# An attention and expert kernel: the expert part is spread in small steps between the turns of the attention loop

## The chip, the cores and the metric

The kernel runs on one core of a Trainium2 chip. The metric is the device time of one execution in microseconds (us). Five engines work side by side, each in the order of its own instruction list, and wait for each other through semaphores: PE (TensorE, matrix multiplies into the accumulators called PSUM, here one tile `ps` of eight banks of 512 f32 columns), ACT (ScalarE), DVE (VectorE), POOL (GpSimd) and SP (SyncE, which here only issues DMAs).

## The reference

For x of 2048 tokens by 128 features, normalised to xn, the output is x plus an attention of 16 heads of 8 features plus a mixture of 8 experts with the top 2 chosen per token.

```python
q, k, v = (proj(W) * mod for W in (Wq, Wk, Wv))              # 16 heads, 8 features each
scores = einsum('bhid,bhjd->bhij', q, k) / sqrt(D)
scores = scores * cos(2 pi (i - j) / S)
w = softmax(scores); w = (w + roll(w, 1, axis=-1)) / sqrt(2)
attn = einsum('bhij,bhjd->bhid', w, v) @ Wo
# experts: a small router picks 2 of 8 per token, each expert is
h1 = x_rep @ w1[e].T; a, g = split(h1); he = silu(a) * g @ w2[e].T     # 704 and 352 hidden
out = x + attn + sum over the two chosen experts of score * he
```

## The kernel before

The cosine factor is folded into the operands: each head has 16 rotated rows for q and for k, written as an f16 high part and an f16 rest to a scratch tensor in DRAM (`qk_parts`) and loaded head by head as 49 rows (`qa`, `ka`). Scores are computed transposed, as 64 tiles a head of 128 keys by 512 queries, 1024 tiles in all. The exponential (ACT, L581) writes a tile in f32 to `probs` (the tensor `big`), and four tiles together (a quad) are multiplied with the values of the head, `vh` (PE, L1098), on four column groups of PE at once.

The work runs in stages, all written out by hand for each engine:

1. The layer norm, the transposes of xn, the router's projection, the values, the expert weights' transposes (24 blocks, PE L926 and L928, taken out by ACT L518 to L521), and the router itself on DVE.
2. The rotated projections (PE L950, DVE L717), their split in two f16 parts (ACT L532, DVE L711), squares (ACT L537) and the stores to `qk_parts` (SP L339). At the same time POOL scatters the token rows, one indirect DMA for each of 32 columns of slots (L444), into expert order (`slots_x`).
3. 39 expert tiles of 128 rows (`run_tiles`). For each: SP loads rows, PE turns them (L959), multiplies with the two halves of w1, 352 columns each (L981, L986), ACT applies Silu (L557), DVE multiplies (L738), PE turns the result (L964), DVE copies it (L733), PE multiplies with w2 (L974), ACT copies (L553), POOL stores to `slots_y`. Stage 3 also holds, beside some tiles, the steps that rank the heads and make the shift rows of the softmax.
4. Attention. PE's loop runs over groups g of three score tiles (`GROUP_OF = 3`, 342 groups): `scores(g)` waits for the exponential of group g-2, then come a `max_job` (only for the two heads that need exact maxima: 128 jobs, 11 a head from head 1, each reduced by DVE L771), and the quads whose tiles are ready. POOL copies the next head's values (`head_values`) and gathers the experts' results beside it.
5. The output projection, the sum, and the stores.

The waits that decide between stages are PE's own order and these:

```python
after(pe, exp_done, g - 1)                       # scores(g)
pe.wait_ge(exp_done, groups_for(tiles[-1] + 1))  # weighted_values(w)
pe.wait_ge(vh_ready, p + 1)                      # first quad of head p
```

Of the kernel before, what the change touches and what calls it, by code (L numbers as in the profile page):

```python
# [30 lines left out]
F32 = mybir.dt.float32  # L31
# [21 lines left out]
TAIL = (GROUPS - 1) * GROUP  # L53
FP = NF * P
ROWS = 2 * D
KQ = 1 + 3 * ROWS
HALF = S // 2
CREDIT = 2
TURNED = 1
GROUP_OF = 3  # L60
RING = 2 * GROUP_OF
PROBS = 5 * GROUP_OF
PER_HEAD = NT * NC
SCORE_TILES = H * PER_HEAD
SCORE_GROUPS = -(-SCORE_TILES // GROUP_OF)
QUADS = PER_HEAD // NC
O_BANKS = (6, 7)
# [3 lines left out]
JOBS_A_HEAD = 11  # L71
JOB_QUAD = 6
ISQ8 = float(1.0 / np.sqrt(D))
# [8 lines left out]
PROJ_BANKS = (4, 5, 0, 1)  # L82
SUM_BANKS = (4, 6, 7, 0)
EARLY = 4
# [3 lines left out]
ONES = 3  # L88
# [3 lines left out]
SQUARES_AT, RANK_AT, ROW_AT, TURN_AT, ORDER_AT = 2, 4, 6, 7, TAIL - 1  # L92


def build(nc, x, Wq, Wk, Wv, Wo, phase, amp, wqkv, w1, w2, ident_in, desc_in, cs_in, sel_in, tri_in, below_in, count_in, heads_in, earlier_in, out):
    scratch = nc.dram_tensor("qk_parts", [2, H, 2, ROWS, S], F16, kind="Internal").ap()
    shift_rows = nc.dram_tensor("shift_rows", [H, S], F16, kind="Internal").ap()
    whole = nc.dram_tensor("whole_qk", [2, H, ROWS, S], F32, kind="Internal").ap()
# [7 lines left out]
    with ExitStack() as ctx:  # L106
# [3 lines left out]
        def sem(name):  # L110
# [7 lines left out]
        probs = big[:].rearrange("p a n -> p (a n)")[:, 0:PROBS * CW].rearrange("p (a n) -> p a n", n=CW)  # L118
        store = sb("store", [P, 10 * S], F16)
        parts = store[:, 0:8 * S].rearrange("p (a b n) -> p a b n", a=4, b=2)  # L120
        attn = store[:, 2 * S:4 * S].bitcast(F32).rearrange("p (t d) -> p t d", d=DM)

# [4 lines left out]
        total = gathered[:, 0, :, :]  # L127
        cs = sb("cs", [P, S], F32)

        hid = cs[:, 0:2 * FP].rearrange("p (a f) -> p a f", a=2)  # L130
        hidT = cs[:, 2 * FP:4 * FP].rearrange("p (a f s) -> p a f s", a=2, f=NF)
# [53 lines left out]
        silu = pair[:].rearrange("p t e j -> p (t e j)")[:, 0:2 * F].rearrange("p (a f) -> p a f", a=2)  # L185
# [33 lines left out]
        proj_ps, rot_ready, v_ps, v_ready, ones_ready = (sem(n) for n in ("proj_ps", "rot_ready", "v_ps", "v_ready", "ones_ready"))  # L219
        hi_ready, parts_ready, scratch_wr = (sem(n) for n in ("hi_ready", "parts_ready", "scratch_wr"))  # L220
# [6 lines left out]
        xgT_ps, xgT_ready, a_ready, g_ready, silu_ready = (  # L227
            sem(n) for n in ("xgT_ps", "xgT_ready", "a_ready", "g_ready", "silu_ready"))
        pad_ready, hid_ready, hidT_ps, hidT_ready, y_ready, y_copied, gather_ld, y_added = (
            sem(n) for n in ("pad_ready", "hid_ready", "hidT_ps", "hidT_ready", "y_ready", "y_copied", "gather_ld", "y_added"))  # L230
# [6 lines left out]
        whole_ld, whole_wr, whole_cs = (sem(n) for n in ("whole_ld", "whole_wr", "whole_cs"))  # L237
# [14 lines left out]
        def run_tiles(eng, tile, beside):  # L252


            for n in range(2 * GROUP):
                tile(n, n % GROUP, False)
                beside(n)
            with eng.Fori(2, GROUPS - 1) as g:
                for k in range(GROUP):
                    tile(g * GROUP + k, k, False)  # L260
            beside(TAIL - 1)
            for n in range(TAIL, TILES):
                tile(n, n % GROUP, n == TILES - 1)
                beside(n)
# [11 lines left out]
        def groups_for(n):  # L276

            return (n - 1) // GROUP_OF + 1
# [9 lines left out]
        def jobs_before(p):  # L288

            return min(max(p - 1, 0) * JOBS_A_HEAD, JOBS)  # L290

# [6 lines left out]
        def _(sp):  # L298
# [10 lines left out]
            for src, at in ((phase, 0), (amp, 1)):  # L309
                for g in range(2):  # L310
                    for half in range(2):
                        sp.dma_start(ang[64 * half:64 * half + 64, at, g:g + 1],
                                     src[8 * g:8 * g + 8, :].rearrange("h (d o) -> (h d) o", o=1)).then_inc(phase_ld, 16)
                sp.dma_start(ang[:, at, 2:3], src.rearrange("h (d o) -> (h d) o", o=1)).then_inc(phase_ld, 16)


            for b in range(2):
                for f, (f0, rows) in enumerate(FCH):
                    sp.dma_start(w1raw[0:rows, NF * b + f, :, :],
                                 w1[:, F * b + f0:F * b + f0 + rows, :].rearrange("e p h -> p e h")).then_inc(w_ld, 16)  # L320
            sp.dma_start(w2raw, w2.rearrange("e p f -> p e f")).then_inc(w_ld, 16)
            for dst, src in ((tri, tri_in), (below, below_in), (count, count_in)):
                sp.dma_start(dst[:], src).then_inc(route_ld, 16)
            sp.dma_start(cs[:], cs_in).then_inc(cs_ld, 16)

# [38 lines left out]
            def load_rows(m, half):  # L364
                after(sp, xgT_ps, m * 2 - 2)
                sp.dma_start(xg[:, 2 * half:2 * half + 2, :], tiles_x[:, bass.ds(m * 2, 2), :]).then_inc(xg_ld[half], 16)

            for i in range(3):
                store_parts(i)
            sp.wait_ge(scattered, 2 * NT * 16)  # L370
            sp.wait_ge(rot_ready, 16)
            for m in range(4):
                load_rows(m, m % 2)
            store_parts(3)
            for m in range(4, 6):
                load_rows(m, m % 2)
            with sp.Fori(3, GROUPS) as g:
                for half in range(2):
                    load_rows(g * 2 + half, half)
# [11 lines left out]
            for r in range(EXACT):  # L391
                load_operands(head_at(PLAIN + r), qe[:, r, :], ka[:, 2 + r, :], exact_ld)
# [832 lines left out]
```

## Time and profile before

| | us |
|---|---|
| median of 3 runs | 709.84 (708.99 to 710.26) |
| the profiled execution, as timed | 707.88 |
| its span, first to last instruction | 706.1 |
| PE busy | 621.4 (88%) |
| ACT busy | 550.1 (78%) |
| DVE busy | 220.7 (31%) |
| POOL busy | 93.3 (13%) |

The page's slices show PE and ACT at nine tenths or more from about 220 us to 690 us, the attention. Before that ACT and DVE are lightly used, and around 60 to 90 us PE does nothing. A busy PE is not a PE at its peak, since the ends of its matmuls are modelled. The profiled execution is 1.96 us (0.3%) under the median; of its 707.88 us, 1.78 us lie outside the span.

### The profile page before, as it was taken

Reading aid. Unit: us, or ns where it says so; the run is one execution under the profiler, and the core shown is the slowest. Engines: PE = TensorE matmul, PEld = TensorE weight load, DVE = VectorE, ACT = ScalarE, POOL = GpSimd, SP = SyncE. Lnnn points to the kernel's source line nnn. Section 1 sums busy time; section 2 is a strip of 40 time slices with the busy share of each in tenths; the row PEclk is TensorE's granted clock in tenths of the full one; section 3 lists DMA queues with packets and bytes.
Section 4 is the critical chain, followed back from the end, with each engine's and each line's share of the span. In section 5 each row is a group of like instructions: output and inputs, shape, how many; then the busy total and the mean of one; then the engine's idle time right before and its main releaser. Section 6 shows DMA issues by size and latency. Waiting matters only on the chain.

```text
span 706.1 us, 11470 instructions
## 1 busy us (share of the span) xinstructions
PE 621.4 (88%) x4151; PEld 201.4 (29%) x4152; DVE 220.7 (31%) x462; ACT 550.1 (78%) x530; POOL 93.3 (13%) x109
## 2 busy tenths in 40 slices
PE   3984057999989999999999999999999999999995
PEld 3841034677751111111111111111111111111113
DVE  7578024334420031423233142331414232005003
ACT  1466024233358999999999999999999999999992
POOL 2038720111110101010010101101010000000000
PEclk9998568899998999999999999999999999999999
DMA  4934321111141101011010101101010010000002
GB/s 129 313 121 148 120 62 66 45 45 59 48 131 47 43 5 46 16 31 36 12 46 1 47 16 31 43 3 46 1 46 25 19 35 1 3 1 1 1 0 63
DMA packets 33828, 34.44 MB, mean 49 GB/s; under 512 B 6092, under 2 KB 27878, under 8 KB 33650
## 3 DMA queue, kind: packets, MB, share of 16 engines
q1 hardware_dynamic: 30786, 27.01, 13.3%
q0 software_dynamic: 2992, 6.76, 2.9%
q8 instruction: 33, 0.54, 0.3%
q14 instruction: 17, 0.14, 0.1%
HBM read 21.14 MB, written 12.58 MB: 48 GB/s over the span
## 4 chain that ended last, share of the span: by engine, by line
PE 60%; ACT 18%; issue 13%; DVE 7%; SPq 2%; DMA 0%; ACTq 0%; DVEq 0%
PE ps L1098 23%; ACT big L581 16%; PE ps L1081 15%; PE ps L981 4%; PE ps L974 4%; PE ps L986 3%; DVE m L771 2%; PE ps L964 2%; SPq L339 2%; PE ps L1116 2%; PE ps L1105 1%; PE ps L915 1%; PE ps L906 1%; DVE big L717 1%; PE ps L959 1%
## 5 line engine op out<-in xcount | busy, mean ns | idle before, releaser
L581 ACT ACTIVATE big<-ps 128x1536 f32<-128x1536 f32 x342 | 471.2, 1459 | 11.9 <-PE ps L1081 4.5
L1098 PE MATMUL ps<-big,vh 128*32 128x512 f32 x2048 | 274.1, 607 | 0.1
L1081 PE MATMUL ps<-qa,ka 49*128 49x512 f16 x896 | 179.8, 385 | 12.2 <-ACT big L581 9.2
L771 DVE TENSOR_REDUCE m<-ps 128x1 f32<-128x512 f32 x128 | 88.5, 692 | 157.5 <-PE ps L1116 157.5
L1081 PEld LDWEIGHTS ps<-qa,ka 49*128 49x128 f16 x896 | 33.1, 93 | 227.1 <-ACT big L581 157.1
L1098 PEld LDWEIGHTS ps<-big,vh 128*32 128x32 f32 x2048 | 40.4, 108 | 103.8 <-issue 98.2
L436 POOL COPY vh<-vaug 128x144 f32 x16 | 5.1, 319 | 382.1 <-PE ps L1098 380.8
L1116 PE MATMUL ps<-ka,attnT 49*128 49x512 f16 x128 | 48.0, 375 | 6.0 <-DVE m L771 5.7
L755 DVE COPY osb<-ps 128x512 f32<-128x512 f32 x16 | 11.1, 692 | 126.7 <-PE ps L1098 126.7
L738 DVE TENSOR_TENSOR cs<-pair,ps 128x352 f32<-128x352 f32 x39 | 20.3, 521 | 85.2 <-PE ps L986 81.6
L553 ACT COPY y<-ps 128x128 f32<-128x128 f32 x39 | 10.4, 266 | 45.6 <-PE ps L974 45.6
L444 POOL DMA_INDIRECT slots_x<-attnT,slot x32 | 36.2, 1133 | 49.6 <-DVE slot L699 40.1
L959 PE MATMUL ps<-ident,cs 128*128 128x128 f32 x39 | 11.4, 293 | 34.6 <-DMA cs<-slots_x 31.4
L981 PE MATMUL ps<-w1T,xgT 128*128 x78 | 33.6, 514 | 5.0 <-issue 2.6
L557 ACT ACTIVATE pair<-ps 128x352 f32<-128x352 f32 x39 | 18.1, 463 | 24.2 <-PE ps L981 24.2
L974 PE MATMUL ps<-w2T,cs 128*128 (+1 forms) x234 | 33.4, 280 | 1.0 <-ACT y L553 0.8
L462 POOL DMA_INDIRECT store<-slots_y,slot x32 | 30.6, 957 | 10.4 <-issue 10.4
L986 PE MATMUL ps<-w1T,xgT 128*128 x78 | 31.7, 490 | 0.0
L974 PEld LDWEIGHTS ps<-w2T,cs 128*128 128x128 f32 (+1 forms) x234 | 29.9, 195 | 1.6 <-issue 1.6
L548 ACT COPY xgT<-ps 128x128 f32<-128x128 f32 x39 | 10.2, 260 | 25.0 <-PE ps L959 25.0
L1081 PE MATMUL ps<-attnT,ka 49*128 49x512 f16 x128 | 25.7, 383 | 2.4 <-ACT big L581 2.4
L762 DVE COPY weight_sums<-ps 128x16 f32<-128x16 f32 x16 | 2.8, 175 | 79.2 <-PE ps L1105 79.2
(165 smaller groups left out, 370.9 us busy)
## 6 DMA issues: line engine op xcount, KB each, us to landing
qk_parts<-store SPq DMA_DIRECT2D x16, 256.0 KB
qa<-qk_parts SPq DMA_DIRECT2D x28, 128.0 KB
slots_x<-vh SPq DMA_DIRECT2D x5, 512.0 KB, 9.1
cs<-slots_x SPq DMA_DIRECT2D x20, 128.0 KB, 2.3
slots_y<-y POOLq DMA_DIRECT2D x19, 128.0 KB, 2.7
store<-in_L_ffn_w SPq DMA_DIRECT2D x4, 512.0 KB, 6.6
ka<-qk_parts SPq DMA_DIRECT2D x32, 64.0 KB, 2.1
qa<-qk_parts SPq DMA_DIRECT2D x28, 64.0 KB
```

Of the source, the lines that this page charges most:

```text
L444: nc.gpsimd.indirect_dma_start(slots_x, bass.IndirectOffsetOnAxis(ap=slot[:, r, t:t + 1], axis=0), xn[:, t, :], None).then_inc(scattered, 16)
L462: nc.gpsimd.indirect_dma_start(gathered[:, r, t, :], None, slots_y, bass.IndirectOffsetOnAxis(ap=slot[:, r, t:t + 1], axis=0)).then_inc(ga ...
L581: nc.scalar.activation(probs[:, first % PROBS:first % PROBS + n, :], ps[:, first % RING:first % RING + n, :], ACT.Exp, scale=ISQ8 / (OPERA ...
L738: nc.vector.tensor_tensor(hid[:, k % 2, 0:F], silu[:, k % 2, :], ps[:, 2 + k % 2, 0:F], ALU.mult).then_inc(hid_ready, 1)
L771: nc.vector.tensor_reduce(m4[:, j // NC, j % NC:j % NC + 1], ps[:, O_BANKS[(p - 1) % 2], :], AX, ALU.max).then_inc(m_reduced, 1)
L959: nc.tensor.transpose(ps[:, 4, 0:P], xg[:, k % 4, :], ident[:]).then_inc(xgT_ps, 1)
L974: ins = nc.tensor.matmul(ps[:, 5, 0:DM], hidT[0:rows, k % 2, f, :], w2T[0:rows, bass.ds(e, 1), f, :].rearrange("p o h -> p (o h)"), start= ...
L981: nc.tensor.matmul(ps[:, k % 2, 0:F], xgT[:, k % 2, :], w1T[:, bass.ds(e, 1), 0:F].rearrange("p o f -> p (o f)"), start=True, stop=True).t ...
L986: nc.tensor.matmul(ps[:, 2 + k % 2, 0:F], xgT[:, k % 2, :], w1T[:, bass.ds(e, 1), F:2 * F].rearrange("p o f -> p (o f)"), start=True, stop ...
L1081: ins = nc.tensor.matmul(ps[:, n % RING, :], k[at:at + KQ, P * o:P * o + P], q[at:at + KQ, CW * c:CW * c + CW], start=True, stop=True, til ...
L1098: ins = nc.tensor.matmul(ps[32 * c:32 * c + 32, O_BANKS[p % 2], :], vh[:, p % 2, o + 8 * b, :], probs[:, n % PROBS, :], start=k == 0, stop ...
L1116: nc.tensor.matmul(ps[:, O_BANKS[(p - 1) % 2], :], qe[at:at + KQ, r, P * i:P * i + P], ka[at:at + KQ, 2 + r, CW * (c % 2):CW * (c % 2) + C ...
```

## The change

The attention loop is moved ahead of the expert work, and the expert work is cut in steps that stand between its turns.

- The loop runs over turns. The first 11 heads (704 tiles) are done in 352 turns of two tiles (`PAIR_RING = 4` banks), the last 320 tiles in groups of three as before. With pairs, banks 4 and 5 are free for the router and the experts.
- Before the first turn stand only the layer norm, the rotated projections with the values between them, the parts, the squares, the head ranking and the loads of heads 0 and 1. The DMAs of the angles go from ACT's queue. SP also keeps a copy of xnT in DRAM (`kept_x`), since `attn` now lies in `xnT`.
- In turns 1 to 4 PE does the rest of the router's projection; DVE runs the router, with its two small exponentials on ACT after groups 12 and 30; after turn 24 PE counts, DVE assigns slots, POOL scatters. In turns 26 to 49 one block of expert weights is turned per turn, and DVE, not ACT, takes it out.
- From turn 70 on, each expert tile has seven turns (`TURNS_A_TILE = 7`, 273 turns for 39 tiles). Step 0: rows are turned. Steps 2 and 3: the two halves of w1 are multiplied with the weights as the stationary side, so the hidden activations come out turned and L964 and L733 fall away. After step 3, ACT makes exp(-a), and DVE makes a/(1+exp(-a)) times g, with a reciprocal. Step 6: the result. The weights of each tile's expert are first copied by SP to one of four staging places (`stage_weights`).
- Max jobs start at head 3, 13 a head, none in steps 4 and 5 of a tile. Gathers stand one to a quad from quad 174.

```diff
-JOBS_A_HEAD = 11
+PAIRED = 11 * PER_HEAD
+PAIRS = PAIRED // 2
+PAIR_RING, PAIR_PROBS = 4, 16
+FIRST_JOB_HEAD = 3
+JOBS_A_HEAD = 13
+RANK_TURN = 24
+WEIGHTS_AT = 26
+EXPERTS_AT = 70
+TURNS_A_TILE = 7
+GATHER_AT = 174
...
+        def expert_step(g):
+
+            m, step = divmod(g - EXPERTS_AT, TURNS_A_TILE)
+            return (m, step) if 0 <= m < TILES else (None, None)
...
+            def decay_of(m):
+
+                act.wait_ge(a_ready, m + 1)
+                after(act, hidT_ready, m - 1)
+                nc.scalar.activation(decay[:, m % 2, :], ps[:, 4, 0:FP], ACT.Exp, scale=-1.0).then_inc(decay_ready, 1)
...
             for g in range(SCORE_GROUPS):
                 weights(g)
...
+                m, step = expert_step(g)
+                if step == 3:
+                    decay_of(m)
...
+            def hidden(m):
+
+                k = m % 2
+                dve.wait_ge(decay_ready, m + 1)
+                then(nc.vector.tensor_scalar(decay[:, k, :], decay[:, k, :], 1.0, BIGGEST, ALU.add, ALU.min))
+                then(nc.vector.reciprocal(decay[:, k, :], decay[:, k, :]))
+                dve.wait_ge(a_ready, m + 1)
+                then(nc.vector.tensor_tensor(decay[:, k, :], decay[:, k, :], ps[:, 4, 0:FP], ALU.mult))
+                dve.wait_ge(g_ready, m + 1)
+                after(dve, y_ready, m - 1)
+                nc.vector.tensor_tensor(hidT[:, k, :, :].rearrange("p f s -> p (f s)"), decay[:, k, :], ps[:, 5, 0:FP],
+                                        ALU.mult).then_inc(hidT_ready, 1)
...
+            def widen(m, b, ready):
+
+                pe.wait_ge(staged_ld[m % STAGES], (m // STAGES + 1) * 32)
+                pe.wait_ge(xgT_ready, m + 1)
+                after(pe, hidT_ready, m)
+                if b == 1:
+                    after(pe, y_copied, m)
+                for f, (f0, n) in enumerate(FCH):
+                    ins = nc.tensor.matmul(ps[0:n, 4 + b, P * f:P * f + P],
+                                           w1_of[m % STAGES][:, F * b + f0:F * b + f0 + n],
+                                           xgT[:, m % 2, :], start=True, stop=True)
+                ins.then_inc(ready, 1)
+
+            def result(m):
+                pe.wait_ge(hidT_ready, m + 1)
...
+            for g, job, quads in turns():
                 if g < SCORE_GROUPS:
                     scores(g)
...
+                if job is not None:
+                    max_job(*job)
+                for w in quads:
                     weighted_values(w)
                     between(w)
...
+                if g == RANK_TURN:
+                    rank_tokens()
+                if weight_block(g) is not None:
+                    turn_weights(weight_block(g))
+                expert_work(g)
```

The order in which the instructions stand moves as follows; `ps` is PSUM, `cs` holds the hidden activations, `xgT` the turned rows, `big` the exponentials, `store` the staged weights.

On PE, in stage 3 of the kernel before, one expert tile stands in a row (w1 in two halves, the next rows, three transposes, the result of the tile two before):

```order
L981 ISA [waits xgT_ready]
L981 MATMUL ps<-w1T,xgT 128x352
L959 MATMUL ps<-ident,cs 128x128 [waits xg_ld0]
L986 ISA
L986 MATMUL ps<-w1T,xgT 128x352
L964 MATMUL ps<-ident,cs 128x128 [waits hid_ready]
L964 MATMUL ps<-ident,cs 128x128 x2
```

On PE in the changed kernel, the end of one tile's seven turns (steps 4 to 6, then step 0 of the next; L1148 is a pair of scores, L1165 a quad, L1091 the result):

```order
L1148 MATMUL ps<-qa,ka 128x512 [waits exp_done]
L1148 MATMUL ps<-qa,ka 128x512
L1148 MATMUL ps<-qa,ka 128x512 [waits exp_done]
L1148 MATMUL ps<-qa,ka 128x512
L1165 MATMUL ps<-big,vh 32x512 [waits exp_done]
L1165 MATMUL ps<-big,vh 32x512 x3
L1148 MATMUL ps<-qa,ka 128x512 [waits exp_done]
L1148 MATMUL ps<-qa,ka 128x512
L1091 MATMUL ps<-store,cs 128x128 [waits hidT_ready]
L1091 MATMUL ps<-store,cs 128x128 x2
L1148 MATMUL ps<-qa,ka 128x512 [waits exp_done]
```

The result of a tile now stands in the attention loop's own list, and the next pair of scores stands behind its wait for `hidT_ready`.

On DVE, in the attention of the kernel before, one head holds this:

```order
L755 COPY osb<-ps 128x512 [waits ot_ready,pv_done]
L759 TENSOR_LOAD head_order
L759 ISA x2
L762 COPY weight_sums<-ps 128x16 [waits ot_ready]
L764 RECIPROCAL rden<-ps 128x16 [waits attn_ready]
L766 ISA [waits rden_ready]
L766 TENSOR_TENSOR store<-ps,rden 128x4x4x8
L771 TENSOR_REDUCE m<-ps 128x1 [waits m_ready] x11
```

On DVE in the changed kernel, each expert tile adds this to the attention (here without max jobs between):

```order
L816 COPY xgT<-ps 128x128 [waits xgT_ps]
L822 TENSOR_SCALAR cs<-cs 128x384 [waits decay_ready]
L823 RECIPROCAL cs<-cs 128x384 [waits dve_step]
L825 TENSOR_TENSOR cs<-cs,ps 128x384 [waits a_ready,dve_step]
L828 TENSOR_TENSOR cs<-cs,ps 128x384 [waits g_ready,dve_step]
L834 COPY y<-ps 128x128 [waits y_ready]
```

Four dependent instructions, one of them a reciprocal over 384 columns, stand between ACT's exponential and the `hidT_ready` for which PE waits.

## Rows read from the trace of the kernel before

**Rows 1.** Busy time by stage: window; its us; each engine's busy us (instructions); clock; DMA.

```profile
91.40:206.50 115.10, 102.70 (x583) 75.53 (x583) 44.47 (x95) 39.18 (x122) 17.13 (x20) 0.92 0.20 62
206.50:690.90 484.40, 464.18 (x3257) 87.82 (x3258) 117.34 (x222) 472.45 (x343) 36.28 (x49) 0.99 0.08 24
```

**Rows 2.** Groups by line: count, busy us, mean ns, idle before, releaser.

```profile
L581 ACT ACTIVATE big<-ps 128x1536 f32<-128x1536 f32 x342 | 471.2, 1459 | 11.9 <-PE ps L1081 4.5
```

**Rows 3.** Timeline, PE at the end of attention: start, us, instruction, count, idle before.

```profile
687.88 0.60 PE L1081 MATMUL ps<-attnT,ka 49*128 49x512 f16 x3
...
688.41 1.07 PE L1098 MATMUL ps<-big,vh 128*32 128x512 f32 x8
...
689.41 0.39 PE L1081 MATMUL ps<-attnT,ka 49*128 49x512 f16 x1
689.72 0.16 PEld L1098 LDWEIGHTS ps<-big,vh 128*32 128x32 f32 x8 [0.23 <-issue]
```

**Rows 4.** The chain that ended last, from 223 us: start, us, what.

```profile
224.72 1.06 ACT big L581
...
226.05 1.26 ACT big L581
```

**Rows 5.** Busy time in two stretches of attention, with and without max jobs.

```profile
340.52:397.80 57.28, 55.30 (x394) 10.24 (x394) 17.23 (x27) 55.97 (x41) 6.28 (x8) 1.00 0.10 28
599.00:690.00 91.00, 87.68 (x613) 16.48 (x609) 12.65 (x45) 89.86 (x67) 0.64 (x2) 1.00 0.00 1
```

**Rows 6.** Timeline, short f32 groups on PE: the expert results, and four transposes.

```profile
202.36 0.83 PE L974 MATMUL ps<-w2T,cs 128*128 x6
...
203.74 0.93 PE L974 MATMUL ps<-w2T,cs 128*128 x6 [0.22 <-ACT y L553]
```

```profile
306.66 0.66 PE L1105 MATMUL ps<-ident,osb 128*128 128x128 f32 x4
307.24 0.11 PEld L1081 LDWEIGHTS ps<-qa,ka 49*128 49x128 f16 x3 [0.17 <-issue]
```

**Rows 7.** Groups by line, the nearest forms to the new ACT and DVE work.

```profile
L738 DVE TENSOR_TENSOR cs<-pair,ps 128x352 f32<-128x352 f32 x39 | 20.3, 521 | 85.2 <-PE ps L986 81.6 <-ACT pair L557 3.6
L557 ACT ACTIVATE pair<-ps 128x352 f32<-128x352 f32 x39 | 18.1, 463 | 24.2 <-PE ps L981 24.2
...
L764 DVE RECIPROCAL rden<-ps 128x16 f32<-128x16 f32 x16 | 4.0, 248 | 0.0
...
L666 DVE RECIPROCAL gate<-gate 128x128 f32<-128x128 f32 x1 | 1.0, 953 | 0.0
```

**Rows 8.** Timeline of POOL: the first of 32 scatters, and the memset behind the last.

```profile
44.40 1.15 POOL L444 DMA_INDIRECT slots_x<-attnT,slot  x1 [40.11 <-DVE slot L699]
...
91.42 3.51 POOL L448 MEMSET attnT<- 128x4096 f16 x1 [1.32 <-DMA slots_x<-attnT,slot]
```

**Rows 9.** Timeline, first uses of PE, projections, squares, head ranking, loads of head 0.

```profile
11.55 2.27 PE L898 MATMUL ps<-ident,attnT 128*128 128x128 f32 x8 [3.57 <-DVE attnT L628]
```

```profile
46.35 9.66 PE L950 MATMUL ps<-xnT,wmat 128*64 128x512 f32 x44
```

```profile
72.19 0.19 ACT L537 ACTIVATION_READ_ACCUMULATOR big<-store 128x1 f32 x1
```

```profile
102.49 0.35 DVE L785 TENSOR_SCALAR sel<-sel,square_sum 128x8 bf16<-128x8 f32 x2
...
104.43 0.58 DVE L790 TENSOR_REDUCE large<-mean_square 128x16 f32<-128x256 f32 x1
```

```profile
117.19 0.16 DVE L798 TENSOR_SCALAR rank<-ps 1x16 f32<-1x16 f32 x1
...
120.94 0.16 DVE L810 TENSOR_SCALAR head_order<-rank 1x16 int32<-1x16 f32 x1
```

```profile
193.31 1.17 SPq L383 DMA_DIRECT2D shift_rows<-shift  x2
...
201.44 0.60 SPq L362 DMA_DIRECT2D qa<-shift_rows  x2
```

More of the change, by code:

```diff
@@ L555, in tile @@
-            def tile(n, k, last):
-                act.wait_ge(a_ready, n + 1)
-                nc.scalar.activation(silu[:, k % 2, :], ps[:, k % 2, 0:F], ACT.Silu).then_inc(silu_ready, 1)
-                if not last:
-                    rows_out(n + 1, k + 1)
-                if not (isinstance(n, int) and n < 2):
-                    results_out(n - 2, k + 2)
-            def beside(n):
-                if n == RANK_AT:
-                    act.wait_ge(square_ready, 1)
-                    nc.scalar.activation(other[:].rearrange("p h t -> p t h"), mean_square[:], ACT.Sqrt, scale=SPREAD * SPREAD).then_inc(other_ready, 1)
@@ L574, in weights @@
             def weights(g):
[L576 to L577 removed]
+                tiles = group_tiles(g)
                 act.wait_ge(score_ready, g + 1)
[L579 to L581 removed]
+                after(act, pv_done, quads_for(held_before(tiles[-1]) + 1))
@@ new lines, in _ @@
+            for half in range(2):
+                nc.vector.tensor_scalar(shift[:, half, :], ps[:, 4, P + P * half:P + P * half + P], -TO_SHIFT, None,
+                                        ALU.mult).then_inc(shift_ready, 1)
+            dve.wait_ge(peak_ps, 1)
+            dve.wait_ge(head_ld, 2 * 16)
+            then(nc.vector.tensor_scalar(rank[:, 0, :], ps[0:1, 3, 0:H], 0.0, None, ALU.max))
+            of_other = rank[:, 0, :].unsqueeze(1).to_broadcast([1, H, H])
+            of_head = rank[:, 0, :].unsqueeze(2).to_broadcast([1, H, H])
@@ new lines, in _ @@
+            for t in range(NT):
+                for g in range(2):
+                    at = t * H + g * 8
+                    ins = nc.tensor.matmul(ps[:, 4, at:at + 8], squares[2 * g][:, P * t:P * t + P], sel16[:, g, :], start=True, stop=True)
+            ins.then_inc(square_ps, 1)
+            pe.wait_ge(large_ready, 1)
+            nc.tensor.transpose(ps[0:H, 2, 0:P], large[:], ident[:]).then_inc(large_ps, 1)
+            pe.wait_ge(other_ready, 1)
+            for half in range(2):
+                ins = nc.tensor.transpose(ps[:, 4, P + P * half:P + P * half + P],
+                                          other[:, 8 * half:8 * half + 8, :].rearrange("p h t -> p (h t)"), ident[:])
```

779 lines of the change are left out of this document (395 added, 384 removed).

## The prediction

> **What bounds the kernel now.** I read the busy time by stage first. The expert tiles take 115.1 us and attention 484.4 us [rows 1]. In attention ACT is busy for 472.45 us and PE for 464.18 us: both are nearly full, so the question is what room PE has. The groups by line give ACT's load: 342 exponentials of three tiles [rows 2]. Undisturbed they start 1.33 us apart (226.05 less 224.72) [rows 4]. The timeline gives PE's: three score tiles hold PE for 0.53 us (688.41 less 687.88), a quad for 1.00 (689.41 less 688.41), a lone score tile for 0.31 (689.72 less 689.41) [rows 3]. Two tiles run on two row groups at once, so a pair also costs 0.31. Four tiles therefore cost PE 4/3 x 0.53 + 1.00 = 1.71 us and ACT 4/3 x 1.33 = 1.77 us. PE has 0.06 us of room in 1.77 us. Without max jobs a group takes 91.0/67 = 1.358 us, with them 57.28/40 = 1.43 us [rows 5]. Expert work that is moved in here is therefore paid on PE almost in full. What the change can win is the time ahead of attention in which PE does nothing useful, and the rest of its gain is overlap of ACT and DVE work that was already hidden.
>
> **Part 1: attention starts early.** Before, the last operand load of head 0 is issued at 201.44 and attention begins about 206.5. In the changed kernel the chain is: PE starts on xn at 11.55 [rows 9], and can project from about 14.5. From the first projection at 46.35 to the last square at 72.38 the kernel before needs 26.0 us [rows 9]; this is set by DVE and ACT, which do the same 16 multiplications, 4 rests and 4 squares. The values' matmuls now stand between the projections on PE; I add 7 us for them, an estimate between 0 (all of it hides under DVE) and 14 (as much again as the 16 projections take on PE, 9.66/44 x 64) [rows 9]: 47.5. From the scale factors to the largest mean square 2.5 us (102.49 to 105.01), then two transposes, the square root and the shift rows, about 1.8 us by their neighbours, then the ranking, 3.9 us (117.19 to 121.10) [rows 9]: 55.7. From the store of the shift rows at 193.31 to the last load of head 0 at 202.04 are 8.7 us [rows 9]; the store starts some 3 us before the ranking is done, so 5.9 us are left, and 2.4 us for the landing: attention starts at **64** (60 to 70). That is 142 us earlier.
>
> **Part 2: turns 0 to 69.** A pair turn costs PE 0.31 + half a quad = 0.81 us. ACT needs two thirds of 1.33 = 0.89 and a little of the fixed part: 0.90, so bare turns take 0.90 us. The 25 turns to the ranking of tokens take 23, with the router's projection and the wait for DVE's chain 25. The scatter then starts near 28 us after the start of attention. Before, from the first scatter to the memset of qe behind them were 47.0 us, and the memset 3.5 [rows 8]. POOL does the values of head 2 only behind that, so PE's first quad of head 2, in turn 65, waits until 28 + 47.0 + 3.5 = 78.5. Without this wait PE would be there at 72: turn 26 at 27.5, 24 turns with three transposes (0.31 + 0.50 + 0.47 = 1.28, the 0.47 by rows 6 below) and 15 bare ones. Behind turn 65 go five turns more. Turn 70 starts at **83**. The wait costs 6 us; it is near zero if nothing disturbs the scatters and 12 if the weight loads disturb them twice as much as the stores did before.
>
> **Part 3: the 39 expert tiles.** PE's own work for seven turns: 7 x 0.31 = 2.17; 3.5 quads, 3.50; three groups of three f32 matmuls. Such a group of six instructions took 0.83 us right behind other f32 work and 0.93 when it had waited, and four transposes took 0.66 while the next weights came 0.58 after their start, so the modelled end overhangs by 0.08 [rows 6]: 0.75 to 0.85, and since each now stands behind f16 or narrow work I take 0.83: 2.49. The rows' transpose 0.28 (0.11 to 0.28). Max jobs: 97 of the 128 fall here, 0.22 each where nothing runs beside (0.53 less 0.31), 0.55 a tile. Turning the output 0.13. The sum is 9.1 us a tile, 355 us in all.
>
> But PE also waits. Take the start of step 3's scores as 0. They end at 0.39, and ACT's exponential of that pair starts at 0.41 and gives way to exp(-a) at 1.31. That one has 384 columns; 352 took 0.463 [rows 7], so 0.49: 1.80. Then DVE: the addition 0.34 (it has a single source, in SBUF; between half and all of the multiplications' 0.56 below); the reciprocal: 16 columns took 0.248 and 128 took 0.953 [rows 7], 6.3 ns a column, so 384 columns take 0.95 + 256 x 0.0063 = 2.56; two multiplications with PSUM, 0.521 for 352 columns [rows 7], 0.56 each. With three gaps of 0.03 that is 4.11, and `hidT_ready` comes at **5.9**. PE has until then four pairs, two quads, one f32 group and a job or so, 1.24 + 2.00 + 0.83 + 0.22 = 4.3. It stands still for 1.6 us, with the next scores behind it, while ACT runs dry. The way back: result 0.83, three pairs 0.93, 1.5 quads 1.50, rows 0.28, first half of w1 0.83, jobs 58/39 x 0.22 = 0.33, turning 0.06: 4.8. One tile is **10.7 us**, all 39 are **417** (395 at the low end of every PE cost, 433 at the high end).
>
> The Trainium skill, "VectorE: DVE Perf Modes", in its walk through the 8-slice pipeline, says that a reciprocal is an iterative divide with a repeat count of 8. By that page's table of modes (2048 f32 columns in 2293 ns at one a cycle) eight cycles would be some 9 ns a column, and by estimate the reciprocal 3.3 us and a tile 11.4. The trace disagrees with it: its two rows give 6.3 ns.
>
> **Part 4: the rest.** Nine pair turns with jobs, 10 us. 320 tiles in groups of three: 40 groups with jobs at 1.43 and 67 without at 1.358 are 148. From the last scores at 689.41 [rows 3] to the end of the span at 706.1 are 16.7, as before. Before, the clock's mean over attention was 0.99 [rows 1], which is about 5 us at half rate, behind a thin stretch of PE work; the new attention begins behind a longer one, and I charge 3 us for it. Removed altogether and at no cost: L964, L733, Silu and two table loads; they lay under PE. The staged weights (two more DMAs a tile, 39 times) lie under SP's idle time; if they came late, each microsecond counts on PE.
>
> **Sum.** 64 + 83 + 417 + 10 + 148 + 16.7 + 3 = 741.7 us of span, 743.5 with the 1.8 us around it, against 707.88. The profiled execution is 0.3% under the median, so 745.5, **745 us**, 5% slower.
>
> **Rivals.**
> 1. PE's costs are at their low ends, since weights are loaded ahead of the next group as in the denser expert stage (against it: a lone pair showed 0.31, no overlap). A tile takes 10.1 us: 39 x 0.6 = 23 less, 722.
> 2. Faster than before: the chain through DVE is covered and PE's own 9.1 us decide. Mechanism: the reciprocal over 384 columns in SBUF is much shorter than the two rows make it, or PE's turns of steps 3 to 6 are long enough by themselves. Then 39 x 1.6 = 62 less: 683. It decides from a tile of 9.8 us on, that is a chain 0.95 us shorter, a reciprocal under 1.6 us. For it: only two reciprocals are in the trace, one reading PSUM. Against it: the slope of 0.705 us for 112 columns is large.
> 3. The chain is 0.7 us longer than worked out, because the reciprocal grows faster beyond 128 columns or DVE comes late to it from a max job. At 11.4 us a tile 39 x 0.7 = 27 more: 772. The page named above would have it so.
> 4. The gain of part 1 and the loss of part 3 meet: a tile of 9.8 us, 709.
>
> **Numbers.** Forecast 0.62 (730 to 760); rival 1 0.14; rival 2 0.12; rival 3 0.08; rival 4 0.04. Range 708 to 774: it leaves out rival 2 and the far side of rival 3. A change of 0.2% is about what a measurement can tell from none. Faster 0.13, same 0.03, slower 0.84.
>
> **What would show it.** The first exponential of the scores near 64 us; the reciprocal's mean near 2.56 us; PE waiting for DVE's last multiplication before L1091, 1.6 us in each tile, some 60 us in the list of waits; ACT busy for only about 75% of the expert stretch, and for over 95% of the last 148 us; expert tiles 10.7 us apart. A first quad of head 2 that waits for POOL shows part 2. The prediction is wrong if the reciprocal is under 1.6 us, if the tiles come 9.8 us apart or less, or if attention starts after 80 us.

## The result: 12.6% slower, and the profile after

| | us, median | lowest to highest |
|---|---|---|
| before | 709.84 | 708.99 to 710.26 |
| after | 799.11 | 797.84 to 800.58 |

The ratio is 1.126 (95% interval 1.124 to 1.128). The forecast was 745, in a range of 708 to 774: the sign was right, the time is 54 us off and outside the range. The profiled execution has a span of 796.0 us, so it is also 54 us above the 741.7 of the sum.

The page of after: busy time, and the span in 40 slices.

```profile
PE 673.1 (85%) x4346; PEld 232.9 (29%) x4346; DVE 367.9 (46%) x648; ACT 534.4 (67%) x535; POOL 77.7 (10%) x91
...
PEclk9965999988989899978899799799999999999998
```

No engine is full any more. The line of the granted clock has 7 or 8 in nine slices spread over the expert tiles (the 8th to the 31st slice), where that of before was at 9 throughout attention but for its first slice. Busy time by stage, which answers to [rows 1] (window, its length, then busy us and instructions of PE, weight loads, DVE, ACT, POOL, then the granted clock, the share of the DMA engines, GB/s):

```profile
67.40:82.60 15.20, 14.88 (x69) 5.24 (x66) 4.23 (x4) 9.79 (x10) 0.00 (x0) 0.58 0.90 214
98.90:131.60 32.70, 31.30 (x222) 11.96 (x222) 16.52 (x45) 23.50 (x26) 23.27 (x25) 1.00 0.19 65
150.30:617.10 466.80, 397.62 (x2509) 153.07 (x2509) 254.23 (x366) 282.88 (x314) 2.55 (x8) 0.91 0.21 71
617.10:629.60 12.50, 9.70 (x69) 2.01 (x68) 4.84 (x7) 8.77 (x10) 1.85 (x2) 1.00 0.07 20
629.60:777.90 148.30, 141.34 (x993) 26.82 (x991) 32.17 (x78) 145.15 (x106) 29.73 (x35) 1.00 0.08 22
```

The windows are cut where ACT starts the exponential of a turn: turn 0 at 67.4, turn 26 at 98.9, turn 50 at 131.6, turn 70 at 150.3, turn 343 (the 39 tiles are over) at 617.1, turn 352 at 629.6, the last at 777.9. The third row holds nearly all of the miss: 39 tiles in 466.8 us, 11.97 us each, with PE busy for 85% of it, ACT for 61%, and a clock of 0.91. The last row, where no expert work is left, is full: ACT 98%.

The groups by line answer to [rows 2, 7]: the exponential, the steps of the chain on DVE, and the expert result that waits for it (count, busy us, mean ns, idle time before and its releasers).

```profile
L618 ACT ACTIVATE big<-ps 128x1024 f32<-128x1024 f32 (+1 forms) x459 | 491.4, 1125 | 217.5 <-PE ps L1148 215.4
L823 DVE RECIPROCAL cs<-cs 128x384 f32<-128x384 f32 x39 | 99.6, 2553 | 1.4
...
L1091 PE MATMUL ps<-store,cs 128*128 128x128 f32 (+1 forms) x234 | 38.4, 303 | 58.1 <-DVE cs L828 58.0
...
L825 DVE TENSOR_TENSOR cs<-cs,ps 128x384 f32<-128x384 f32 x39 | 21.6, 554 | 1.3
...
L611 ACT ACTIVATE cs<-ps 128x384 f32<-128x384 f32 x39 | 18.9, 485 | 0.0
...
L822 DVE TENSOR_SCALAR cs<-cs 128x384 f32<-128x384 f32 x39 | 14.0, 360 | 82.5 <-ACT cs L611 82.5
```

One tile, from step 3 on, in the timeline of all engines (start, us, instruction; in brackets the idle time before it and what ended it):

```profile
299.88 1.02 ACT L618 ACTIVATE big<-ps 128x1024 f32<-128x1024 f32 x1 [0.37 <-PE ps L1148]
...
300.80 0.48 ACT L611 ACTIVATE cs<-ps 128x384 f32<-128x384 f32 x1
...
301.72 2.55 DVE L823 RECIPROCAL cs<-cs 128x384 f32<-128x384 f32 x1
...
304.89 0.55 DVE L828 TENSOR_TENSOR cs<-cs,ps 128x384 f32<-128x384 f32 x1
...
305.50 0.94 PE L1091 MATMUL ps<-store,cs 128*128 128x128 f32 x6 [1.52 <-DVE cs L828]
306.37 0.39 PE L1148 MATMUL ps<-qa,ka 49*128 49x512 f16 x2
...
306.80 1.02 ACT L618 ACTIVATE big<-ps 128x1024 f32<-128x1024 f32 x1 [1.67 <-PE ps L1148]
```

Read it from the bottom: ACT runs dry for 1.67 us because the scores behind L1091 in PE's queue come late; L1091 came late because it waited 1.52 us for DVE's last multiplication; and that one stands behind the reciprocal. This is the chain that the prediction described. So the mechanism is there, and the question for the experiments was what made it cost 50 us more.

### The profile page after: what moved, and what is told of

It is laid out like the page before. It is cut to its first block, busy times and chain, and to the rows that moved or that the text cites. A ratio compares the mean times of both kernels' runs of the same rounds, so it can differ in the third digit from the quotient of the medians.

```text
span 796.0 us, 11999 instructions
## 1 busy us (share of the span) xinstructions
PE 673.1 (85%) x4346; PEld 232.9 (29%) x4346; DVE 367.9 (46%) x648; ACT 534.4 (67%) x535; POOL 77.7 (10%) x91
## 4 chain that ended last, share of the span: by engine, by line
PE 48%; DVE 23%; ACT 12%; issue 11%; SPq 2%; DMA 2%; ACTq 1%; DVEq 0%
PE ps L1165 17%; DVE cs L823 12%; PE ps L1148 11%; ACT big L618 9%; PE ps L1082 5%; PE ps L1091 5%; PE ps L1183 3%; DVE cs L825 3%; DVE cs L828 3%; DVE m L871 2%; ACT cs L611 2%; DVE cs L822 2%; PE ps L986 2%; PE ps L1072 1%; PE ps L1025 1%
## 5 line engine op out<-in xcount | busy, mean ns | idle before, releaser
L618 ACT ACTIVATE big<-ps 128x1024 f32<-128x1024 f32 (+1 forms) x459 | 491.4, 1125 | 217.5 <-PE ps L1148 215.4
L1165 PE MATMUL ps<-big,vh 128*32 128x512 f32 x2048 | 291.8, 644 | 0.4 <-ACT big L618 0.4
L1148 PE MATMUL ps<-qa,ka 49*128 49x512 f16 x896 | 176.2, 404 | 16.6 <-DMA qa<-shift_rows 8.3
L823 DVE RECIPROCAL cs<-cs 128x384 f32<-128x384 f32 x39 | 99.6, 2553 | 1.4
L1148 PEld LDWEIGHTS ps<-qa,ka 49*128 49x128 f16 x896 | 38.8, 94 | 173.0 <-ACT big L618 101.1
L1091 PE MATMUL ps<-store,cs 128*128 128x128 f32 (+1 forms) x234 | 38.4, 303 | 58.1 <-DVE cs L828 58.0
L1082 PE MATMUL ps<-xgT,store 128*128 128x128 f32 (+1 forms) x468 | 80.0, 312 | 2.7 <-DMA store<-w2T 2.7
L1082 PEld LDWEIGHTS ps<-xgT,store 128*128 128x128 f32 (+1 forms) x468 | 62.1, 199 | 54.7 <-issue 51.7
L1165 PEld LDWEIGHTS ps<-big,vh 128*32 128x32 f32 x2048 | 41.2, 110 | 92.2 <-issue 81.1
L1183 PE MATMUL ps<-ka,attnT 49*128 49x512 f16 x128 | 51.5, 402 | 11.1 <-DVE m L871 11.1
L1091 PEld LDWEIGHTS ps<-store,cs 128*128 128x128 f32 (+1 forms) x234 | 30.7, 200 | 82.3 <-DVE cs L828 81.9
L822 DVE TENSOR_SCALAR cs<-cs 128x384 f32<-128x384 f32 x39 | 14.0, 360 | 82.5 <-ACT cs L611 82.5
L1148 PE MATMUL ps<-attnT,ka 49*128 49x512 f16 x128 | 25.3, 383 | 2.2 <-ACT big L618 2.2
L816 DVE COPY xgT<-ps 128x128 f32<-128x128 f32 x39 | 11.2, 288 | 26.9 <-PE ps L1072 26.9
L834 DVE COPY y<-ps 128x128 f32<-128x128 f32 x39 | 11.4, 292 | 23.6 <-PE ps L1091 23.5
L825 DVE TENSOR_TENSOR cs<-cs,ps 128x384 f32<-128x384 f32 x39 | 21.6, 554 | 1.3
```

Source lines behind the costliest of these rows:

```text
L618: nc.scalar.activation(probs[:, prob_of(tiles[0]):prob_of(tiles[-1]) + 1, :], ps[:, bank_of(tiles[0]):bank_of(tiles[-1]) + 1, :], ACT.Exp, ...
L822: then(nc.vector.tensor_scalar(decay[:, k, :], decay[:, k, :], 1.0, BIGGEST, ALU.add, ALU.min))
L823: then(nc.vector.reciprocal(decay[:, k, :], decay[:, k, :]))
L825: then(nc.vector.tensor_tensor(decay[:, k, :], decay[:, k, :], ps[:, 4, 0:FP], ALU.mult))
L1082: ins = nc.tensor.matmul(ps[0:n, 4 + b, P * f:P * f + P], w1_of[m % STAGES][:, F * b + f0:F * b + f0 + n], xgT[:, m % 2, :], start=True, s ...
L1091: ins = nc.tensor.matmul(ps[:, 5, FP:FP + DM], hidT[0:n, m % 2, f, :], w2_of[m % STAGES][0:n, f, :], start=f == 0, stop=f == NF - 1)
```

## Experiments

Three things are to be told apart: the length of DVE's chain, TensorE's clock as a consequence of the stops, and PE's own work for a tile. Times below are medians of four executions with the 95% interval of the ratio to the kernel before, which took 708.2 to 709.1 us in all four sets of runs. "Tiles" is the time from turn 70 to turn 343, "half clock" the time at 1.2 GHz within it; both, like the column of turns 26 to 50, are from the one profiled execution. The first two rows are one kernel, and differ by 7 us in the whole, 5.5 us in the tiles and 10 us of half clock: so much the clock's part can vary by itself.

| kernel | us | ratio | turns 26 to 50 | tiles | one tile | half clock in tiles |
|---|---|---|---|---|---|---|
| after | 799.1 | 1.126 | 32.7 | 466.8 | 11.97 | 85 |
| e5_after_again | 792.3 | 1.118 (1.115 to 1.122) | 34.1 | 461.3 | 11.83 | 75 |
| e1_tanh | 732.0 | 1.032 (1.030 to 1.035) | 68.6 | 366.5 | 9.40 | 0 |
| e7_tanh_again | 696.9 | 0.983 (0.981 to 0.986) | 34.1 | 366.6 | 9.40 | 0 |
| e2_recip128 | 738.5 | 1.043 (1.041 to 1.046) | 68.7 | 372.6 | 9.55 | 0 |
| e9_recip256 | 771.7 | 1.088 (1.085 to 1.091) | 68.8 | 408.7 | 10.48 | 14 |
| e3_fill | 798.8 | 1.129 (1.126 to 1.132) | 69.0 | 434.5 | 11.14 | 0 |
| e4_late | 814.1 | 1.149 (1.145 to 1.152) | 69.1 | 448.3 | 11.50 | 82 |
| e6_tanh_paced | 699.6 | 0.988 (0.985 to 0.990) | 32.7 | 370.2 | 9.49 | 7 |
| e10_tanh_mix | 728.5 | 1.027 (1.025 to 1.030) | 69.0 | 366.5 | 9.40 | 0 |
| e8_tanh_warm | 730.7 | 1.031 (1.029 to 1.033) | 68.7 | 366.7 | 9.40 | 0 |
| e12_mix_again | 728.8 | 1.028 (1.026 to 1.030) | 69.5 | 366.4 | 9.40 | 0 |
| e11_mix_paced | 696.4 | 0.983 (0.981 to 0.984) | 33.0 | 365.3 | 9.37 | 0 |

The column of turns 26 to 50 holds a surprise of its own, 35 to 36 us that came in some sets of runs and not in others. It is taken up behind the chain; until then only the tiles are compared, which it leaves alone (e1_tanh and e7_tanh_again are one kernel, with and without it: 366.5 and 366.6).

### The chain taken away: e1_tanh

```
-  activation(decay, a, ACT.Exp, scale=-1.0)
+  activation(decay, a, ACT.Tanh, scale=0.5)
...
-  decay = min(decay + 1, BIGGEST); decay = 1 / decay; decay = decay * a
-  hidT = decay * g
+  decay = (decay + 1) * a;  hidT = (decay * 0.5) * g
```

> The same result by another formula: ACT makes tanh(a/2) in place of exp(-a), and DVE makes (tanh + 1) * a and then half of that times g, two instructions in place of four, no reciprocal. DVE's chain before the last semaphore falls from 4.12 us to about 1.2 us. Theory A (PE stands 1.5 us a tile for DVE, 58 us in all, and these stops are also what lets the TensorE clock fall to half in the expert stretch, some 30 us more): a tile falls from 11.9 us to about 9.7, the clock of the expert stretch returns to 1.0 and the whole takes 705 to 720 us. Theory B (the clock falls for another reason, the many short f32 groups): the wait goes, the clock stays near 0.91, 735 to 745 us. If a table were loaded between tanh and exp, ACT would pay 2.6 us a tile and the time would stay above 780 us.

The chain on DVE shrinks to two instructions of 0.554 us. The tiles take 366.5 us, 100 less, PE waits for L826 nowhere, and the clock is 1.00 throughout, as theory A had it (9.40 us a tile, 9.7 expected). The total of 732.0 lies above its 705 to 720 for the stall in turns 26 to 50 that is told below. No table is loaded between tanh and exponential.

```profile
185.60:552.10 366.50, 357.32 (x2509) 143.52 (x2509) 142.30 (x288) 281.88 (x314) 2.55 (x8) 1.00 0.27 90
```

PE does the same 2509 matmuls as in after, busy for 357.3 us of 366.5, where it was busy for 397.6 of 466.8. So 40 us of the 100 were PE busy for longer with the same work, as a lower clock makes it, and 60 us were PE standing. (The clock is worth somewhat less than 40 in time, since work that takes longer also fills part of the waits; e3_fill below prices it.) The row also checks the prediction's sum of PE's own work: 357.3/39 = 9.16 us a tile, where it had 9.1. The other 0.24 us of the 9.40 are idle time, most of it a max job that waits for the maximum of the job before it (8.2 us in the 39 tiles of e7_tanh_again, the same kernel).

### The chain shortened: e2_recip128 and e9_recip256

```
-  reciprocal(decay[:, k, :], decay[:, k, :])
+  reciprocal(decay[:, k, 0:P], decay[:, k, 0:P])          # e2: 128 of 384 columns
+  reciprocal(decay[:, k, 0:2 * P], decay[:, k, 0:2 * P])  # e9: 256 of 384 columns
```

The other columns are left without their reciprocal in both.

> The reciprocal runs over 128 of the 384 columns, the rest is left as it is (so the experts' hidden values are wrong there). DVE's chain is 1.6 us shorter, 2.5 us against 4.1, by nothing but its size. Theory A: the wait of 1.5 us a tile is just covered and the clock recovers, 715 to 735 us. Theory B: the wait goes, the clock does not, 740 to 750 us. If DVE's chain is not what decides the stretch: within 10 us of 799.

> The changed kernel with the reciprocal taken on 256 of the 384 columns (the other 128 are left without it, so the output is not the reference's): the chain is 0.85 us shorter than in the changed kernel, 0.85 longer than with 128 columns. Theory A (the wait and the half clock are two costs, and the clock falls only where the stops are long enough): the warm tile falls from 11.1 to about 10.2 us, and nearly all of the half clock goes, so the 39 tiles take about 400 us (against 467 with all columns and 373 with 128), the kernel 725 to 735 us where no stall falls in turns 26 to 50, 36 more where one does. Theory B (the clock falls with any stop): the half clock stays at about 90 us of the 39 tiles, which take about 435 us, the kernel 760 us.

The reciprocal takes 953 ns on 128 columns, 1753 on 256, 2553 on 384: 6.25 ns a column, near the 6.3 that the two rows of [rows 7] gave.

```profile
L823 DVE RECIPROCAL cs<-cs 128x256 f32<-128x256 f32 x39 | 68.4, 1753 | 1.4
```

The tiles go 9.55, 10.48, 11.97. The chain with 0.95 us of reciprocal costs 0.15 us a tile more than the tanh's: nearly all of it is covered, and the clock is 1.00 (theory A of e2; without the 36 us of the stall its 738.5 would be 702, below the 715 to 735 expected). The next 0.80 cost 0.93 and bring back a little half clock (3 of 39 tiles). The last 0.80 cost 1.49. Tiles in which the clock stayed at full tell the two apart: 10.34 us in e9 (36 tiles), 11.21 in after (20 tiles). The full-clock tile thus grows by 0.87 for 0.80 of chain, about one for one, as a chain on the critical path must, and the rest of the 1.49 is clock. In e9 theory A expected 400 us and hardly any half clock, theory B 435; 408.7 with 14 us of half clock is much nearer to A. The step is no cliff, but it is steep.

### The stops filled: e3_fill

```
+  pe.wait_ge(exp_done, g)
+  for _ in range(12):
+      transpose(ps[:, bank_of(first_of(g + 1)), 0:P], ident, ident)
   result(m)
```

The twelve transposes stand ahead of each expert result and are read by nothing.

> Twelve f32 transposes of the identity into the next pair's PSUM bank are put on PE ahead of each tile's result, where it stands still; nothing reads them. They take 1.3 us, about what the wait takes, so no wait on the chain gets shorter. Theory A (the stops let the clock fall): the clock of the expert stretch rises to about 1.0 and the time falls by 20 to 30 us, to about 770 us, although PE has more to do. Theory B (another cause): clock 0.91 and 799 us or a few more.

This is the run that settles the part of the clock. The edit adds a wait for an exponential too (PE stood 6.7 us for it in all). PE is given more to do, 468 transposes, in the place where it stood still, and DVE's chain is left at its length:

```profile
184.50:619.00 434.50, 414.90 (x2977) 193.42 (x2977) 254.11 (x366) 282.61 (x312) 2.56 (x8) 1.00 0.22 76
```

The clock is 1.00 where it was 0.91, and the tiles take 434.5 us instead of 466.8: PE does more and is done 32 us sooner (27 against e5_after_again, the same kernel as after). A tile takes 11.14 us, near the 11.21 of after's full-clock tiles. So the stops of 1.5 us in a tile had lowered the clock, and that costs 27 to 32 us; the chain's own part of the loss, 39 x (11.14 - 9.40) = 68 us, is untouched. It is not the set of runs: e4_late, in the same set, has its stops and a clock of 0.91. The total was the same as after's, and not the 770 of theory A, only because turns 26 to 50 took 36 us more here.

### The result moved a turn: e4_late

```
-  elif step == 6: result(m)        # PE, and result_out(m) on DVE
+  result of tile m in step 0 of tile m + 1, ahead of its rows
```

> Each tile's result stands one turn later, in step 0 of the next tile ahead of the turned rows; all else is as in the changed kernel, the four DVE instructions too. One more turn of PE's work (0.3 us, or 1.3 with a quad, plus a max job) covers the chain, so the wait falls from 1.5 us to about 0.6 a tile. Theory A: 25 to 40 us for the wait and part of the clock back, 745 to 765 us. Theory B: 765 to 775 us, clock 0.91.

The wait did not go away, it moved, and the tiles still took 448.3 us at a clock of 0.91. (The profiled execution took 820.0 us, 5.9 above the median of 814.1. Less the 36 us of the stall the median would be 778, near theory B; theory A missed.) The list of PE's waits says where (engine and line waited for, us in total, times, longest):

```profile
PE ps L1188 <- DVE m L876: 39.5, 31, 2.0
...
PE ps L1096 <- DVE cs L833: 12.9, 10, 1.5
```

The wait for the hidden rows falls from 58.0 to 12.9 us, but the next max job (L1188) now waits for the maximum of the job before it (L876), which stands in DVE's queue behind the 2.55 us reciprocal. After's figure for that pair is 11.1. DVE is in order: here the reduction behind the reciprocal inherited the wait.

### Turns 26 to 50: a stall that comes with some sets of runs

In the first set (e1 to e4) all four kernels took 69 us there, where after's own trace has 32.7. So after itself was run again, with e1_tanh's twin and a version that spaces the scatters.

> The changed kernel once more, unchanged. In the four runs so far that kept its order of work, turns 26 to 50 took about 69 us where the changed kernel's own trace has 32.7 us: all engines but GpSimd stood nearly still from about 107 to 147 us, while GpSimd issued its 32 scatters, and the 16 KB fetch of instructions that the changed kernel's trace has at 113.8 us came only at 148. Theory A (the stall belongs to the chip or the placement in memory, not to the edit): here the changed kernel itself shows the stall and takes about 799 + 36 = 835 us. Theory B (it belongs to the edited kernels): 799 us again, turns 26 to 50 in 33 us.

> e1_tanh once more, as the run to compare the paced kernel with on one chip. If the stall in turns 26 to 50 belongs to the kernel, 732 us again; if it belongs to the chip or to the placement of the program in memory, it may be gone, and then the kernel takes 732 - 36 = 696 us.

> e1_tanh with the 32 scatters paced: scatter i waits for 13 + 5i/8 finished sets of four score tiles, so that at most one is issued per 1.25 turns, and the copy of the third head's values stands among them. Theory A (the stall comes from the scatters being issued in one unbroken burst, 1.23 us each, so that the fetch of instructions waits behind it): the fetch now comes through between two scatters, turns 26 to 50 take about 33 us instead of 69, and the kernel about 732 - 36 = 696 us, faster than before (709). Theory B (any scatter under way holds the fetch, or the stall has another cause): it stays at 730 us or more, with the stall as long as the last scatter is out.

None of the three stalled: e5 792.3 us, e7 696.9, e6 699.6. The stall belongs neither to the edits nor to after: the same kernel takes 732.0 in one set and 696.9 in another, and the difference is that of turns 26 to 50 (34.5 us of 35.1). e7 also shows that with the chain gone, and no stall, the changed order takes 1.7% less than the kernel before. With no stall in its twin, e6 left the question of pacing open. It took 2.7 us more than its twin; its trace has 6.8 us of half clock at the start of the tiles that e7's has not. The question was asked again, on a kernel that moves the router's mixes too:

```
-  MIX_BEFORE = 8
+  MIX_BEFORE = NT                       # e10, e12, e11, e8: all 16 ahead of turn 0
...
+  for _ in range(20): transpose(...)    # e8 only: ahead of the squares' sums, and behind the mixes
```

```
   for r, t:                             # e6 and e11: 32 scatters, i = NT * r + t
+      w = 13 + 5 * i // 8
+      pool.wait_ge(pv_done, w)
+      if w >= QUADS, once: head_values(2)
       indirect_dma_start(slots_x, ...)
```

> e1_tanh with all 16 mixes ahead of the first turn, without the idle transposes. Theory A: the 8 mixes (1.05 us a turn at half clock, 4.2 us in all) leave the turns that TensorE bounds, and the kernel takes 2 to 4 us less than e1_tanh, 693 to 695 us (36 more where the stall falls); the clock stays at half in turns 0 to 10. Theory B: the turns are bound elsewhere: no difference.

> e1_tanh with all 16 mixes of the router ahead of the first turn instead of 8 (they stand in TensorE's wait for the operands, 58 to 66.9 us), and 20 + 20 transposes of the identity that nothing reads, in the two waits of TensorE ahead of attention (43.5 to 51.4 us, and behind the mixes). Theory A (turns 0 to 10 take 14.7 us instead of some 9.5 because the clock is at half after these two waits, 0.59 in 67 to 82 us, and because of the 8 mixes among them): they take about 10 us, and the kernel 5 us less than e1_tanh, 692 us (728 where the stall falls). Theory B (the start is bound by ScalarE's exponentials or by loads): no difference.

> e10_tanh_mix with the 32 scatters paced as in e6_tanh_paced (scatter i waits for 13 + 5i/8 finished sets of four score tiles). Whether the stall of turns 26 to 50 falls has gone by sets of runs so far: every changed order in the first and third set had it, none in the second. Theory A (a scatter is issued each 1.26 us without a pause, and it is the unbroken row that starves the other engines' supply in such a set): with the stall in its unpaced twin (728 us) this one is free of it, 693 to 696 us. Theory B (each scatter under way does it, whatever the gap): in such a set it stalls too, 728 us or more. In a set without the stall both take 693 to 695 us, and this is left open.

> e10_tanh_mix once more, the unpaced twin. Where the stall falls 728 us as before; where not, 728 - 36 = 692 us, which would be 4 to 5 us less than e7_tanh_again and 16 less than the kernel before: the 8 mixes moved into TensorE's wait for the operands (turns 0 to 10 in 11.6 us instead of 14.7).

e10, e8 and e9_recip256 ran in a set that stalled (728.5 and 730.7 for the first two), e11 and its unpaced twin e12 side by side in another. There e12 stalled (728.8) and e11 did not (696.4, where 693 to 696 was expected). One window of each, 107 to 145 us, first e12_mix_again, then e11_mix_paced:

```profile
107.00:145.00 38.00, 8.14 (x32) 2.71 (x36) 3.22 (x7) 5.47 (x6) 26.37 (x26) 0.50 0.13 49
```

```profile
107.00:145.00 38.00, 33.77 (x239) 10.34 (x239) 9.40 (x25) 29.93 (x32) 24.89 (x26) 0.99 0.15 54
```

In the stall PE issues 32 matmuls in 38 us instead of 239, and POOL alone keeps its pace. The longest waits in that window of e12 are put down to nothing that the profile shows ("remote" and "issue" name no instruction of another engine):

```profile
ACT big L618 <- remote: 36.5, 3, 24.2
DVE w1T L808 <- issue: 24.7, 1, 24.7
PEld ps L1023 <- issue: 23.7, 3, 20.5
```

PE, ACT and DVE all stand; shorter waits for each other stand between (PE for ACT's exponentials 6.2 us, for DVE 3.1). An obvious suspect is the supply of instructions. The records of the DMA queue that fetches them (16 KB at a time; fetches from 86 to 157 us) fit it in part: in most kernels with the stall no fetch starts from before the scatters until they are over.

```
kernel           fetches of the 16 KB queue, start in us    first and last scatter, us
after            95.0  113.8  131.9  153.6                  101.0 to 140.3
e7_tanh_again    94.8  114.8  133.2  154.5                  100.6 to 140.0
e1_tanh          94.6  148.4                                100.5 to 139.8
e9_recip256      95.1  148.6                                100.9 to 140.4
e8_tanh_warm     86.5  103.5  156.9                          95.9 to 135.2
```

The last row speaks against it: e8_tanh_warm has a fetch early among its scatters and stalled all the same, and its PE runs again from 142 us on, 15 us before the next fetch. So a late 16 KB fetch does not explain the stall by itself; the fetches may as well be late because the engines stand. What is shown: the stall covers nearly the stretch of the unbroken row of 32 scatters, issued every 1.26 us (in e12 they are issued from 96.3 to 135.6, and PE all but stands from 105 to 142); in one set it fell on the unpaced kernel in all its executions (728.05 to 729.83) and on the paced one in none (695.23 to 697.16). That is one pair. Of the eleven runs with the unpaced row eight stalled, and of the two with the paced row none; whether the stall belongs to a whole set or falls on each kernel anew was not tested, and in the second case a pair like this can be chance. Why a run has it or not stays open; the kernel before never showed it (its times are the same in all sets), and its 32 scatters are issued from 44 to 90 us, before attention.

The mixes behaved as expected in size: turns 0 to 10 take 11.6 us in e10 and 10.6 in e12 (one kernel) where e7 has 14.6, and e10 as a whole takes 3.5 us less than e1_tanh. e8, whose clock in 67 to 82 us is 0.77 against 0.69 in e10, takes 11.6 too. The idle transposes raised the clock a little and gained nothing: theory A of e8 was wrong in that half. What is left there is not PE's clock; the share of the DMA engines in the window is 0.94 in e8, while the loads and the stores of the operands run, but no experiment took them away.

## Why the prediction failed, step by step

**Part 1, start of attention: 64 predicted, 67.4 measured.** Within its bounds (60 to 70), 3.4 us of the miss.

**Part 2, turns 0 to 69: 83 predicted, 82.8 measured,** but by luck: two errors meet. Turn 26 started at +31.4 instead of +27.5: in the first 15 us PE was busy for 14.88 of 15.20 at a clock of 0.58, with the router's mixes among the turns (moving the mixes out, in e10 and e12, gave back 3 to 4 us of this). And the weight turns took 32.7/24 = 1.36 us instead of 1.28. PE thus came to the first quad of head 2 at about the time when POOL had its values ready: the memset of qe ends and the copy begins at 146.05, 78.6 after the start (predicted 78.5), and PE's wait there, 6 us in the forecast, is nil. POOL was timed well; what waits for it was not.

**Part 3, the expert tiles: 417 predicted, 466.8 measured. This is the step that failed.** Its mechanism was right: reciprocal 2.553 us (2.56), exp(-a) 0.485 (0.49), addition 0.360 (0.34), multiplications 0.554 (0.56), the last multiplication done 5.99 us after the start of step 3's scores at 299.45 in the tile shown (5.9), PE's wait 58.0 us in the list, 1.49 a tile (1.6). Two terms were short, and the second, which the sum had at nothing for the tiles, is the larger:

- The tile at full clock, 11.21 us instead of 10.7: 39 x 0.5 = 20 us. Counted from step 3's scores to the next step 3's, the 20 tiles at full clock take 11.13 us on average, 6.09 to the start of the result (5.9 forecast, with its small delays between engines) and 5.04 from there (4.8). Most of the latter 0.24 is a wait that the sum did not have: a max job stands until DVE has the maximum of the job before it, 7.9 us in the tiles, 0.2 a tile.

```profile
PE ps L1183 <- DVE m L871: 7.9, 18, 0.7
```

The f32 groups were sized nearly right: the timeline gives a group 0.93 to 0.94 us, but the next scores start 0.87 after it (306.37 less 305.50), against 0.83 in the sum.

- The clock. The sum charged half rate for 3 us, once, at the start of attention, and let the tiles run at 1.00, since before had 0.99 there [rows 1]. But before's PE hardly stood in attention (464.18 us busy of 484.4), and the forecast itself put a stop of 1.6 us in each tile. The same rows held a hint: the clock was 0.92 over before's own expert stage, whose trace has 10.2 us at half clock in its midst, from 119.9 us on. PE was at half clock for 85 us of the tiles, in pieces of 3.4 to 10.2 us; tiles that such a piece touches take 12.8 us instead of 11.2. With 39 x 0.76 this is 30 us. e3_fill, which fills the stops, takes 32 us less. Without this term the kernel would have taken some 769 us, inside the range.

**Part 4.** The last 320 tiles 148.3 (148); nine pair turns 12.5 (10); from the last exponential to the end 18.1 (16.7, which was counted from the last scores). The 3 us charged for a cold start appear in no place of their own; the half clock at the start lies inside part 2.

The miss adds up: 3.4 - 0.2 + 49.8 + 2.5 + 0.3 + 1.4 - 3.0 = 54.2.

**The rivals.** Rival 2 (faster, 683, when the chain is covered) named the right switch: with the chain gone e7_tanh_again takes 696.9, 14 more than its figure, of which 12 are the tile of 9.40 for 9.1 (mostly the max jobs' waits again). Its point of decision, a reciprocal under 1.6 us, was too generous: with 1.75 us a tile takes 10.48, with 0.95 it takes 9.55, and a line between them crosses 9.8 at 1.17. Rival 3 (772, the chain 0.7 longer) came nearest in time, for the wrong reason: the reciprocal did not grow faster, and the chain was 0.2 us longer, not 0.7. The estimate that the walk through the 8-slice pipeline in "VectorE: DVE Perf Modes" of the Trainium skill led to, 3.3 us for the reciprocal, is refuted by 2.553 us over 39 of them.

**The range** took bounds for every duration of an instruction and none for the rate at which PE would run. A bound was in reach: 85 us at half rate was not foreseeable, but tiles at half clock for a good part of their time would have been an upper end well past 774.

## What to carry to other kernels

When an edit makes TensorE stop regularly, the price is the stop and, where the granted clock falls with it, also slower matmuls around it: here 58 us of waiting came with 85 us at half clock, which cost another 30 us or so. With stops of half the length (e9_recip256) it was 14 us at half clock, and with next to none (e2_recip128, 4.4 us in all) nothing. Look at the granted clock of such a stretch before trusting a sum, or take the wait away: two DVE instructions on a tanh, in place of an exponential, an addition, a reciprocal and two multiplications, turned the changed order from 12.6% slower to 1.7% faster in a run without the stall of turns 26 to 50 (e7; e11_mix_paced, which also moves the mixes and spaces the scatters, 696.4 us, ratio 0.983 with 0.981 to 0.984). With the stall the same kernel is 3.2% slower (e1). And before moving a long instruction past a wait, read who stands behind it on its own engine: a later place for the expert result handed much of the wait for the reciprocal's 2.55 us to the max jobs.

## What the runs showed of the hardware

- TensorE's granted clock fell to half in the midst of dense work, with stops of 1.5 us in tiles of 11 us: 0.91 over 467 us, 0.86 in the worst quarter. With stops of about half that (e9_recip256, 32.9 us in 39 tiles) it was 0.98, and with no stop (e1_tanh) or a filled one (e3_fill) 1.00.

```profile
230.00:350.00 120.00, 100.59 (x679) 38.89 (x672) 73.27 (x104) 75.44 (x84) 0.64 (x2) 0.97 0.20 68
350.00:470.00 120.00, 105.28 (x631) 40.26 (x632) 63.51 (x94) 69.69 (x77) 0.65 (x2) 0.86 0.20 68
```

The two rows, of after, are both amid the tiles, with nearly the same kind of work. The second has 0.86 of the clock, is busy for 105.3 us against 100.6, and gets 631 matmuls done instead of 679. Busy time alone is no measure of work done here.

- The f32 reciprocal on DVE was linear in its columns, 6.25 ns each from 128 to 384, with 0.15 us fixed; it took 4.6 times the multiplication of the same width (2553 against 554 ns, the latter with one source in PSUM).
- While POOL issued an unbroken row of 32 indirect scatters, PE, ACT and DVE stood nearly still, at a cost of 35 to 36 us, in eight of eleven runs; the same scatters with pauses did not show it in the one pair that tells. That the scatters cause it is not shown.
